# A Flamingo block on one core: first and second half of the exponentials waited for apart, and a new order of five ring buffers

## The reference

```python
x = x + tanh(g_xattn[0]) * attention0(layernorm(x), ctx, mask)   # 16 heads of 32, 154 keys, projection out
x = x + tanh(g_ffn[0])   * moe(layernorm(x))                     # shared expert + 64 experts, top 8
x = x + tanh(g_xattn[1]) * attention1(layernorm(x), ctx)         # 16 heads of 32, 154 keys
x = x + tanh(g_ffn[1])   * fused_experts(layernorm(x))           # two branches of low-rank experts with a running sum

def moe(h):                                     # h: 4096 x 512
    gu = h @ shared_gate_up_w                   # 512 x 2048
    shared = silu(gu[:, :1024]) * gu[:, 1024:] @ shared_down_w * sigmoid(h @ shared_gate_w)
    ...                                         # softmax, top 8 of 64, 256 slots an expert
    return y + shared
```

## Time and profile before

| what | value |
| --- | --- |
| median of 3 runs | 2900.51 us (2896.17 to 2910.41) |
| time of the profiled execution | 2895.59 us |
| span of the profiled execution | 2893.8 us |
| TensorE matmul busy | 2703.5 us (93%) |
| VectorE busy | 1642.1 us (57%) |
| ScalarE busy | 1526.5 us (53%) |
| GpSimd busy | 1037.9 us (36%) |
| mean granted TensorE clock | 0.986 of full |

### The profile page before, as it was taken

How to read it: one execution, slowest core, us unless ns; L and a number is a source line. 1 busy time by engine, 2 the same in 40 slices (tenths; PEclk the granted TensorE clock), 3 DMA queues, 4 the chain that set the end, 5 groups by cost and what they waited for, 6 DMA issues and landing times. The chain is left out here.

```text
span 2893.8 us, 47205 instructions
## 1 busy us (share of the span) xinstructions
PE 2703.5 (93%) x18014; PEld 1529.9 (53%) x18014; DVE 1642.1 (57%) x2727; ACT 1526.5 (53%) x3658; POOL 1037.9 (36%) x823
## 2 busy tenths in 40 slices
PE   6988988999999989999999889888999999999999
PEld 4554544444444457777777555555444444444444
DVE  7788885655555356556566478887553322343332
ACT  5888895323323146666666389988443222332231
POOL 2444452365555646666666401011102111220111
PEclk9999999999999999999999999999999999999999
DMA  4011103211111269999999701101510000000000
GB/s 153 20 54 49 49 16 130 78 45 45 48 48 36 75 201 283 286 289 289 274 288 286 206 20 42 48 31 32 173 48 1 30 29 13 17 30 30 15 1 30
DMA packets 152272, 277.75 MB, mean 96 GB/s; under 512 B 19952, under 2 KB 28912, under 8 KB 152048
## 3 DMA queue, kind: packets, MB, share of 16 engines
q1 hardware_dynamic: 115184, 207.39, 20.5%
q0 software_dynamic: 36864, 67.34, 11.1%
HBM read 198.86 MB, written 75.89 MB: 95 GB/s over the span
## 5 line engine op out<-in xcount | busy, mean ns | idle before, releaser
L1402 POOL DMA_INDIRECT ids<-sh_tk,sh_su x256 | 271.0, 1059 | 259.7 <-PE sh_gu L53 89.8
L53 PE MATMUL ex_gu<-ex_xT,ex_h 128*128 128x256 f16 x3072 | 345.8, 273 | 3.5 <-issue 2.7
L53 PEld LDWEIGHTS ex_gu<-ex_xT,ex_h 128*128 128x128 f16 x3072 | 300.4, 98 | 52.0 <-issue 3.3
L1741 POOL DMA_INDIRECT xp<-ex_oo,ex_to x128 | 240.0, 1875 | 180.1 <-ACT ex_oo L1682 135.0
L2318 POOL TENSOR_TENSOR fe_prodT<-fe_pp,fe_prodT 128x512 f16<-128x512 f32 x64 | 76.8, 1199 | 604.4 <-ACT fe_prodT L2082 604.4
L522 PE MATMUL at_g<-id,at_p 128*128 128x128 f32 x1280 | 209.1, 290 | 66.6 <-POOL at_p L914 25.0
L1536 DVE SCALAR_TENSOR_TENSOR ex_h<-ring,ex_h 128x1024 f16<-128x1024 f32 x128 | 151.1, 1222 | 154.7 <-ACT ex_h L1526 154.7
L522 PEld LDWEIGHTS at_g<-id,at_p 128*128 128x128 f32 x1280 | 164.9, 170 | 138.7 <-issue 39.7
L688 ACT ACTIVATE at_s<-at_s,at_mx 128x154 f32<-128x154 f32 x512 | 210.4, 417 | 0.1
L913 POOL TENSOR_TENSOR at_p<-at_s,at_rs 128x1024 f32<-128x1024 f32 x64 | 121.5, 1898 | 239.7 <-DVE at_rs L812 239.7
L2226 DVE SCALAR_TENSOR_TENSOR ring<-fe_g,fe_nf,ring 128x512 f32<-128x512 f32 x32 | 24.0, 750 | 293.1 <-PE fe_g L1987 293.1
(11 more groups left out here) (328 smaller groups left out, 5685.8 us busy)
## 6 DMA issues: line engine op xcount, KB each, us to landing
ring<-L_ffn_expert_gate_up_w SPq DMA_DIRECT2D x64, 1024.0 KB
ring<-L_ffn_expert_down_w SPq DMA_DIRECT2D x64, 512.0 KB
ring<-x SPq DMA_DIRECT2D x24, 1024.0 KB, 5.7
x<-ring SPq DMA_DIRECT2D x16, 1024.0 KB, 5.3
zrows<-hm_zs SPq DMA_DIRECT2D x32, 256.0 KB
xp<-ring SPq DMA_DIRECT2D x8, 1024.0 KB
ring<-xp SPq DMA_DIRECT2D x8, 1024.0 KB, 5.7
out<-ring SPq DMA_DIRECT2D x8, 1024.0 KB, 4.2
```

The costliest lines, as they stand in the source:

```text
L53: mm = nc.tensor.matmul(out, lhs(a, k), rhs(b, k), start=start and i == 0 and j == 0, stop=stop and i == n - 1 and j == 2)
L1402: e.indirect_dma_start(ids, bass.IndirectOffsetOnAxis(slotu[b % 2][:, t, j:j + 1], 0), pair[b % 2][:, t, j, :], None, bounds_check=SLOTS - ...
L1741: e.indirect_dma_start(dst, bass.IndirectOffsetOnAxis(to[:, n:n + 1], 0), o32[y % 2][:, t, :], None, bounds_check=T + SLOTS - 1, oob_is_er ...
```

## The change

In the second attention TensorE waits ahead of the first four transposes of a unit for the first half of its exponentials only (`expd` at 2i + 1); the wait for both halves (2i + 2) now stands behind the step's first piece, ahead of the second four transposes.

The shared expert's pieces take three slots in turn where they took four. The ring order of `Shared.x` is changed so that block 1's rows have the buffer of the first attention's block 7. Pieces 3 and 4 are loaded by SyncE during the end of the first attention (`sync_next`), once `w_lo` is 1 and 3, ahead of its wait for the last block's results and their store. After the barrier SyncE waits for that store and loads the rows of block 1 first; piece 5 is loaded after `ids`, once `w_lo` is 4. All later stages have their ring buffers renamed (4 to 1, 1 to 0, 0 to 2, 2 to 4) and keep their relations.

```diff
--- before.py
+++ after.py
@@ -256,7 +256,7 @@
 
         self.nc, self.I, self.layer, self.s, self.src = nc, I, layer, s, src
         sb = lambda n, s_: ctx.enter_context(nc.sbuf_tensor(f"at{layer}_{n}", s_, F32))
-        self.x = [ring[i] for i in ((1, 0, 2, 3, 4) if layer == 0 else (0, 4, 1, 3, 2))]
+        self.x = [ring[i] for i in ((1, 0, 2, 3, 4) if layer == 0 else (2, 1, 0, 3, 4))]
         self.wq32 = self.x[1]
         self.wk = self.x[2 if layer else 4]
         self.wv, self.wq, self.homes = wv if layer else sb("wv", [P, KT, D]), homes.w, homes
@@ -608,11 +608,13 @@
                     mm.then_inc(s["s_mm"], 1)
                 i = n - behind
                 if 0 <= i < UNITS:
-                    e.wait_ge(*((s["prob"], i + 1) if L0 else (s["expd"], 2 * i + 2)))
+                    e.wait_ge(*((s["prob"], i + 1) if L0 else (s["expd"], 2 * i + 1)))
                     keys_turned(i, 0, 0)
                 for what in plan[n][:1]:
                     piece(*what)
                 if 0 <= i < UNITS:
+                    if not L0:
+                        e.wait_ge(s["expd"], 2 * i + 2)
                     keys_turned(i, 4, 1)
                 for what in plan[n][1:]:
                     piece(*what)
@@ -942,6 +944,8 @@
                         e.wait_ge(s["lim_got"], B)
                         mask(B)
                 elif what == "finish" and k == TPB - 1:
+                    if rows_ahead and B == NB - 1:
+                        rows_ahead.sync_next()
                     e.wait_ge(s["x_out"], TPB * B + TPB)
                     e.dma_start(dst[B * BLK:(B + 1) * BLK, :].rearrange("(t p) d -> p t d", p=P),
                                 nrm.block(B)[:, :, :]).then_inc(s[f"st{B % NX}"], 16)
@@ -979,7 +983,7 @@
         nc.all_engine_barrier(sem_only=True)
 
 
-SH_SEMS = (Norm.SEMS + " st0 st1 st2 st3 st4 zst0 zst1 zst2 zst3 cleared ids_in wg_in w_in0 w_in1 w_in2 w_in3 w_hi w_lo tri iota own"
+SH_SEMS = (Norm.SEMS + " st0 st1 st2 st3 st4 zst0 zst1 zst2 zst3 cleared ids_in wg_in w_in0 w_in1 w_in2 w_hi w_lo tri iota own"
            " lg_mm lg_sub ex_out sg_out chosen pos_mm pos_far pos_set eq route gu_mm silu a ahi alo f_mm x_out")
 
 
@@ -991,9 +995,9 @@
 
     def __init__(self, nc, ctx, K, I, ring, s, src, homes):
         self.nc, self.I, self.s, self.src, self.homes = nc, I, s, src, homes
-        self.x = [ring[i] for i in (3, 0, 2, 4, 1)]
+        self.x = [ring[i] for i in (3, 2, 4, 1, 0)]
         self.nrm = Norm(nc, ctx, "sh", s, K, self.x, homes)
-        self.slots = [ring[i] for i in (4, 1, 0, 2)]
+        self.slots = [ring[i] for i in (4, 1, 0)]
 
         self.scat = [ctx.enter_context(nc.semaphore(f"sh_scat{i}")) for i in range(2)]
         up = I["L0_ffn_shared_gate_up_w"].rearrange("(k p) n -> p k n", p=P)
@@ -1020,7 +1024,7 @@
 
     def staged(self, i):
 
-        return self.slots[i % 4], (self.s[f"w_in{i % 4}"], 16 * (i // 4 + 1))
+        return self.slots[i % 3], (self.s[f"w_in{i % 3}"], 16 * (i // 3 + 1))
 
     def sync_piece(self, i):
         slot, (landed, _) = self.staged(i)
@@ -1032,6 +1036,12 @@
                                ).then_inc(self.s["wg_in"], 16)
         for i in range(3):
             self.nc.sync.wait_ge(*before.stored(4 + i))
+            self.sync_piece(i)
+
+    def sync_next(self):
+
+        for i, split in ((3, 1), (4, 3)):
+            self.nc.sync.wait_ge(self.s["w_lo"], split)
             self.sync_piece(i)
 
     def stored(self, b):
@@ -1417,14 +1427,12 @@
                             ).then_inc(s[f"zst{n % 4}"], 16)
 
             e.wait_ge(*before.stored(NB - 1))
-            H.sync_piece(3)
+            nrm.sync_load(1, src)
             for t in range(TPB):
                 keep_rows(t)
             e.wait_ge(s["cleared"], 1)
             e.dma_start(ids.rearrange("(p n) a -> p (n a)", p=P), empty).then_inc(s["ids_in"], 16)
-            e.wait_ge(s["w_lo"], 1)
-            H.sync_piece(4)
-            e.wait_ge(s["w_lo"], 3)
+            e.wait_ge(s["w_lo"], 4)
             H.sync_piece(5)
             sync_clear(nc, before.s)
 
@@ -1436,7 +1444,6 @@
                     e.wait_ge(s["w_lo"], 3 + b)
                 nrm.sync_load(b, src)
 
-            rows(1)
             for b in range(NB):
                 if b + 2 < NB:
                     rows(b + 2)
@@ -1482,8 +1489,8 @@
         self.w1 = sb("h1_0", [P, 2, KT, 2 * EI], F16)
         self.w2 = sb("h2_0", [P, 2, EI // P, D], F16)
         self.xgot = [sems.enter_context(nc.semaphore(f"ex_x{i}")) for i in range(self.NG)]
-        self.st1 = [ring[i] for i in (4, 1, 3)]
-        self.st2 = [ring[0][:, 0:2, :], ring[0][:, 2:4, :], ring[2][:, 0:2, :]]
+        self.st1 = [ring[i] for i in (1, 0, 3)]
+        self.st2 = [ring[2][:, 0:2, :], ring[2][:, 2:4, :], ring[4][:, 0:2, :]]
 
     def sync_first(self, x):
         self.nc.sync.dma_start(self.st1[x % 3][:, :, :], self.I["L0_ffn_expert_gate_up_w"][x, :, :]
@@ -1786,8 +1793,8 @@
 
         self.gen = ctx.enter_context(nc.psum_tensor("fe_g", [P, 2, 512], F32))
         self.early = homes.zT, h0[:, :, :].bitcast(F16).rearrange("p k (h n) -> p h k n", h=2)
-        self.x = [ring[i] for i in (4, 3, 2)]
-        self.cz = [ring[i] for i in (1, 0)]
+        self.x = [ring[i] for i in (1, 3, 4)]
+        self.cz = [ring[i] for i in (0, 2)]
         self.stage = (self.x[1], self.x[2], self.cz[1])
 
     def wide(self, n):
```

## The result

The changed kernel takes 2886.93 us (median of 10 runs), the kernel before 2900.64 us in the runs beside it: ratio 0.9953 [0.9942, 0.9965]. It is faster by 13.7 us; the interval leaves out no change, but the gain stays just under the 14.5 us (0.5%) that the prediction set as its line. The forecast was 2880, and 17.3 us off the profiled execution.

What follows compares the result with a forecast made beforehand. TensorE, busy 93% of the span, bounds the kernel; ScalarE paces the second attention. 6.2 + 0.8 + 4.0 + 0.75 + 5.6 = 17.3 us off the profiled execution is 2878.3; predicted 2880, range 2866 to 2893.

Steps and rivals of the forecast that it cites:

- Shared expert: 6.2 forecast: Block 0: earlier rows remove TensorE's 4.61 us stall and 2.89 of half clock, less a new 1.3 wait: 6.2 us.
- the new wait of 1.03: Shared expert, near 529: TensorE was to wait 1.3 us for VectorE's low half, for block 1's last tile.
- Steady blocks: the step that failed: Second attention: earlier transposes, then projection, scores and copy, remove waits of 0.41 and 0.36; 0.8 us a block, 4.0 for five.
- 0.8 for the first block: Second attention's first block, ScalarE full and two projections at its end: gain of 0.8 us, bounds 0 and 1.2.
- The wait foreseen for VectorE's maximum: Steady blocks: the copy's 0.81 us wait was to turn into ScalarE's exponentials waiting for VectorE's maximum.
- Last block: 6.35 forecast: Second attention's last block, without rows to make: 0.75 us from the first eight waits and 5.6 from the other ten.
- 2.6 more: Last block: extra gain if the steps about 2000 ran at full clock; left out of the sum.
- its eight waits: Last block's first eight waits, with projections and the bank, 5.7 us in all: gain of 0.75 us.
- the seven waits and the 1.7: Last block: seven waits of 0.37 to 0.86 go whole, 3.5 us; three at half clock about 2000 give 1.7.
- VectorE takes the place of the wait: Rival: VectorE paces nearly everywhere in the second attention, which gives about 5 us; sum 11, 2885 us; chance 0.18.
- TensorE's lead lasts: Rival: second attention's copies no longer wait, two thirds of 31.9 us gained, full clock in the last block; 2868; chance 0.12.
- The last rival: Slower: TensorE works in a lump, then idles longer in the second attention's sparse steps, clock falls; 2911 us; chance 0.04.

Runs made afterwards that it cites:

- the run with the last query parts: Changed kernel, but VectorE, not ScalarE, copies the last two of a block's four query parts from block 2 on, second attention; ratio 0.9961 to the kernel before.
- part 2: Changed kernel with the wait for both exponential halves ahead of the step's first piece, so only the first four transposes run early; ratio 0.9946 to the kernel before.
- the run with the first query parts: Changed kernel, but VectorE copies the first two of a block's four query parts from block 2 on, second attention; ratio 0.9962 to the kernel before.
- the first pair: The first profiled executions of the kernel before and the changed kernel, both unaltered; medians 2900.64 and 2886.93 us.
- the first set: Follow-up runs of each half of the change alone and both kernels again, unaltered; the changed kernel took 2873.42 us, ratio 0.9960.
- the third set: A later group of runs beside the kernel before (2905.9 us), with the changed kernel repeated unaltered; its ratio 0.9969.

## Why the forecast held, and where it was off

The time came out 2886.9, in the range, and 3.6 us short of the forecast gain by medians (13.7 against 17.3). The prediction gave a gain of more than 14.5 us a chance of 0.63 and one within it 0.33; 13.7 lies within, by a little.

**Shared expert: 6.2 forecast, 6.3 and 5.9 measured.** Each step stands in the trace: the rows ready, the stall of 4.61 gone, the clock at 1.00 behind it, the new wait of 1.03 (on ScalarE's copy, with VectorE's low half 0.1 us ahead of it). The early pieces, taken as free, did delay nothing; that they were worth anything was not seen. Without them 1.9 us of the gain are lost.

**Steady blocks: the step that failed.** "The projection behind starts earlier, and with it the next scores, transposes and the copy that waited 0.36." It did not start earlier, since its bank was not free. The prediction named the bank at the values but did not look for it at the query parts. Up to the first store shown the forecast had 0.8 for the first block and 0.8 for a steady one, and got 0.25 (87.28 against 87.03 us); of 3.2 for the next four it got 0.63 (178.39 against 177.76 us). The wait foreseen for VectorE's maximum is small, 1.4 us in 3 waits over the stage where it was 0.5 in one (it limits what a further edit can take, as the run with the last query parts shows). That the missing gain sat in the bank is shown by the trace (0.54 of some 0.6 us at that place) and borne out by the blocks of 43.7 us in the two runs in which VectorE frees it; the forecast had 43.8. Those runs also relieve ScalarE of two copies, so they don't measure the bank alone.

**Last block: 6.35 forecast, 6.7 measured,** and this near hit is two errors that cancel. The clock did not fall near 2000, which was priced at 2.6 more, so 9 should have come. The first stretch, with its eight waits (to the copy at 1979.25, before at 1981.44), gave 0.5 (0.75 forecast). The ten steps to the last copy gave 6.6, where the seven waits and the 1.7 made 5.2, or 7.8 with the clock. At the end 0.4 were expected, but from the last copy on it takes 0.5 longer (17.3 against 16.8 us); why was not looked into. Some of the lead is taken by banks again (waits of 0.33 at 1983.65 and 1999.93). In the kernel before, TensorE had stood still 1.67, 0.75 and 1.13 us between its pieces before and around the fall; in the changed one 1.45 and 1.34, and the transposes stand without a wait behind the scores. The Trainium skill ("TensorE: Matmul & The Clock Gate", Part 4) says that transposes do not count as work for the gate; by that the half clock should have stayed. The trace does not bear out this use of it: transposes came earlier and the clock held. No run here splits that from the shorter idle time. With the second wait ahead of the piece (part 2) 3.4 us of half clock come back at 2002.

**The rivals.** "VectorE takes the place of the wait" had the size (2885, and 2886.9 is nearer to it than to 2880), not the mechanism. "TensorE's lead lasts" fell to the banks. The last rival, a fall of the clock in sparse steps, did not come in the steady blocks of the changed kernel, but it is real: with the banks freed it cost 1.53 us in each steady block (4.28 against 2.75), in every other one, or in one of four. The Trainium skill (the same page, Part 1) has the gate fall when the engine has idled. The 1.97 us of idling ahead of the fall go the same way; but in the run with the first query parts the same two gaps, 0.97 and 0.71 us, brought a fall in one block and none in the next, so their length does not settle it.

**The size of the whole.** In the first pair the spans differ by 8.3: 13.9 from the two stages, 0.5 at the start, less 6.0 in blocks 1, 2 and 7 of the shared expert, which the change does not touch. In the first set, where those gaps are absent, it is 13.2 by the spans (2884.3 and 2871.1) and by the medians alike.

## What to carry to other kernels

A wait that is taken from an engine lets it reach the next instruction early; ask for that one which buffer it writes and when its last reader comes. Here it was a PSUM bank freed behind eight exponentials, and the wait moved by one instruction. An engine that arrives early and then idles also risks its clock: price the next stall at the half-clock duration of the work behind it (here 4.28 us for 2.75). And look for that clock before a difference of 1 to 2 us is put down to an edit: here 3.4 us of it moved within the last block between kernels and was worth 1.6. Compare stages, not spans, when two profiled executions differ where the change has no part.

## What was not expected of the hardware

In block 1 of the shared expert some sets of runs have gaps and others have not, with one kernel. The changed kernel in the third set, with them, and in the first, without: ScalarE's timelines.

```profile
575.58 1.28 ACT L1225 ACT_TABLE_LOAD   x1
580.25 0.60 ACT L1225 ACTIVATE sh_si<-sh_gu 128x512 f32<-128x512 f32 x1 [3.39 <-PE sh_gu L53]
```

```profile
574.00 1.28 ACT L1225 ACT_TABLE_LOAD   x1
575.30 0.60 ACT L1225 ACTIVATE sh_si<-sh_gu 128x512 f32<-128x512 f32 x1
```

The first activation behind the table load is 3.39 us late in the one and immediate in the other, with the same work around it. VectorE stands behind ScalarE (5.11 us), TensorE behind VectorE (3.73 us ahead of 583.78), and TensorE's next 24 matmuls take 7.00 us, not 5.34, with 3.4 us at the half clock from 584.2. In the profiled execution at the top the same place has 3.11 us with another releaser named. What held ScalarE was not found, and no run was aimed at it.

The experts' stage, which no edit touches, varied between 631.8 and 647.3 us over the runs; TensorE waits there for gathered rows, and this was not looked into either.
